# A segment maximum rewritten from chunks and a late gather into a walk over groups and blocks, with 244 steps in an attention walk and another order of two fronts

## The chip, the cores and the metric

The kernel runs on one core of a Trainium2 chip. The metric is device time in microseconds (us), the median of several runs. The engines are TensorE (PE in the rows, PEld its weight loads), VectorE (DVE), ScalarE (ACT), GpSimd (POOL) and SyncE (SP); each works through its own queue of instructions in order, and semaphores join them. Both ScalarE and SyncE also issue DMAs here, and GpSimd issues every indirect DMA (gathers and scatters by a list of row numbers).

## The reference

A graph network of four layers on N = 6250 nodes with D = 128 features and E = 100000 edges. Edges are sorted by `dst`, which is drawn as `floor(6250 * u**2)`, so that low nodes have many edges and high ones few; `src` is random.

```
h = relu(layernorm(x));  x = x + log_softmax(sage(elu(sage(h))))          # two SAGE convolutions, segment means over dst
h = relu(layernorm(x));  x = x + batchnorm(h1 + ffn(h1)),  h1 = batchnorm(h + gat4(h))   # 4 heads, mean over heads
h = relu(layernorm(x));  x = x + prelu(gat2(h))                           # 2 heads of 64
h = relu(layernorm(x));  x = x + relational(h)

def relational(h):                    # the last layer
    msg[e] = h[src[e]] @ W[rel[e]] + b[rel[e]]          # 4 relations
    agg = segment_max(msg, dst);  agg = 0 where a node has no edge
    return h @ W[4] + b[4] + agg
```

An attention layer scores each edge from a term of its source and one of its target, takes a softmax over the edges of each target and sums the weighted sources.

## The kernel before

**Sizes.** P = 128. Nodes are NT = 49 blocks (`tiles`) of 128. The padded edge list has ET = 784 tiles of 128 edges. GT = 7 tiles make a group (GE = 896 edges); there are GN = 112 groups. A *walk* goes through the pairs of group and node block that meet in the sorted list: SN = GN + NT − 1 = 160 steps. Each step has one group of gathered rows and one block of nodes; it moves on either to the next group or to the next block. GpSimd gathers the groups into a ring of RG = 8 groups, and a group's place is freed when its last step has used it.

**The stages.** (1) Two SAGE walks (`walk_pass`, line 899) of 160 steps; GpSimd gathers from `h_tab`, then from `sage_tab` (L919). Per step DVE builds a one-hot of targets (L1056) and PE sums the rows by it, 14 matmuls (L1194). `group_col` and `block_col` hold each step's group and block per partition, for the two table gathers after group LAP = 2, and `retire_walk` the step at which each group's place comes free. (2) A first front (`project`, line 585, with `front` at 1489 and `post` at 1500): in 7 groups of 7 blocks it subtracts the logarithm, takes the layernorm and multiplies by the score weights; `nodeval` receives the products, and GpSimd scatters them, one of 49 scatters per block, into `start1_rows` (L620). (3) The first attention walk (from line 1600) goes by groups of QT = 4 tiles: QN = 196 groups, QN + NT − 1 = 244 pairs, rounded up to QS = 248 steps in QWN = 31 windows of QW = 8. SP stores each finished block to `gat_tab` and `total_tab` (L1646), one store pair for each of the 248 steps. (4) Batchnorm and feed-forward. (5) The second attention's front (`front` at 2400, `post` at 2404), in which ScalarE takes the square root (L830) and the normalised rows and copies the products out; scatters again at L620. (6) The second attention walk. (7) The last front (2853) and products, which write `y_tab`, the rows of all four relations' products for every node. (8) The last pass.

**The order inside `project`.** DVE makes the norms of groups 0 and 1. Then, in each step i, with `starts` given (stages 2 and 5), it waits for product(i), copies it in `post` and then makes norm i + 2; without `starts` (stage 7) norm i + 2 comes first (lines 633 to 638). PE's `turn` of group i + 1 stands before the product of group i (stage 2) or in its middle (stages 5 and 7). In stage 2 the products of seven blocks fill one PSUM area in turn; in stages 5 and 7 four banks take one block's product each (`banks`, line 595).

**The last pass before** (`edge_pass`, line 397, called at 2880). The 784 tiles go in CT = 4 at a time, 196 chunks, in an unrolled loop over NB = 4 buffers. Per chunk, ScalarE copies four columns of `y_idx` to `slot` (L514), which lets GpSimd gather four tiles of `y_tab` (L422); PE transposes them into `pa` (L495); DVE runs a segmented maximum along the edges (L471), where `mask` is a row from `cut_row` that starts each segment anew; PE transposes it back (L505), ScalarE copies it (L525) and issues the write of 512 rows to `scan_rows` (L531). The mask is loaded by SP. Behind the whole loop GpSimd gathers, for each block, the row of every node's last edge from `scan_rows` (`gather_results`, line 549, L557, indices `last_idx`), DVE adds groups of seven blocks to `x` (L2890) and SP stores them (L2899).

The core of it:

```
for t in range(CT):                                    # PE, L495
    ins = nc.tensor.transpose(to, rows(s, t), ident[:, :])
...
v.tensor_tensor_scan(scan_t[:, b, :], mask[:, c, :], pa[:, b * CE:(b + 1) * CE],
                     scan_t[:, 1 - b, CE - 1:CE], op0, op1)          # DVE, L471
```

`last_idx`, the index of each node's last edge, is made between the two SAGE walks in a small block that also makes `start_idx` (from line 1443).

## Time and profile before

| | us |
|---|---|
| median of 3 runs (lowest, highest) | 5873.93 (5870.14, 5876.07) |
| the profiled execution's own time | 5876.16 |
| its span | 5874.4 |
| busy in the span: PE / PEld / DVE / ACT / POOL | 3278.1 / 2756.8 / 2906.4 / 1827.9 / 3903.4 |
| granted TensorE clock, mean over the span | 0.728 |
| first SAGE walk, first gather starts | 58.0 |
| first front, first scatter starts | 2099.3 |
| last pass, first gather of `y_tab` starts | 4816.0 |
| last pass, last gather of `y_tab` starts | 5793.4 |

How to read it: the span is what the profiler recorded of one execution, from its first to its last instruction; the execution's own time holds the 1.8 us around it. Busy times are sums over the whole kernel and mix stages with different limits, so no engine's share says by itself what a stage waits for. The granted clock is a share of 2.4 GHz; 1.0 and 0.5 are TensorE's two levels, and a mean between them is a mixture in time.

### The profile page before, as it was taken

The page shows a single profiled execution, that of the slowest core. Times are in us where ns is not written, and L with a number is a line of the kernel's source. Part 1 is how long each engine was busy: PE and PEld are TensorE (multiplying, and loading weights), DVE is VectorE, ACT ScalarE, POOL GpSimd, SP SyncE. Part 2 cuts the span into 40 slices and gives each one's busy share as a digit, 9 for nine tenths or more (in the row PEclk, how much of TensorE's full clock was granted, in tenths as well). Part 3 has the DMA queues.
Part 4 walks back from the last instruction along what each step waited for, and adds up shares of the span by engine and source line. Part 5 has one row for each costly group of instructions (what it writes and reads, how often), then busy time and mean ns, then how long its engine had stood idle before and what let it go on. Part 6 is the DMA issues. An engine that isn't in the chain of part 4 may idle for free. (4 is left out here: it accounts for less than half of the span.)

```text
span 5874.4 us, 89970 instructions
## 1 busy us (share of the span) xinstructions
PE 3278.1 (56%) x15772; PEld 2756.8 (47%) x15773; DVE 2906.4 (49%) x7625; ACT 1827.9 (31%) x6493; POOL 3903.4 (66%) x4083
## 2 busy tenths in 40 slices
PE   3444555545555525889999894244555563334332
PEld 3444455444555523677777644233445533333331
DVE  4233344434455656788888852344555652222221
ACT  2111111111122213666666653233344441111110
POOL 4777777677777747777776003777777517777776
PEclk9667777766677756999999995566677785555555
DMA  4222222211111112344444211222222134444443
GB/s 122 61 62 63 63 65 66 72 53 52 53 53 52 53 41 78 111 113 117 119 117 113 95 46 31 52 53 54 53 53 52 38 111 130 133 132 130 131 133 107
DMA packets 441899, 474.71 MB, mean 81 GB/s; under 512 B 131954, under 2 KB 337214, under 8 KB 441695
## 3 DMA queue, kind: packets, MB, share of 16 engines
q0 software_dynamic: 130464, 264.37, 17.1%
q1 hardware_dynamic: 184116, 146.31, 8.3%
q10 hardware_dynamic: 127227, 63.09, 3.6%
q14 instruction: 69, 0.57, 0.0%
q8 instruction: 23, 0.38, 0.0%
HBM read 315.46 MB, written 157.97 MB: 81 GB/s over the span
## 5 line engine op out<-in xcount | busy, mean ns | idle before, releaser
L1194 PE MATMUL pa<-arena,weighted 128*128 x4480 | 860.0, 367 | 855.8 <-POOLq L913 511.2
L1194 PEld LDWEIGHTS pa<-arena,weighted 128*128 128x128 f32 x4480 | 795.4, 273 | 909.4 <-issue 909.2
L422 POOL DMA_INDIRECT arena<-y_tab,slot x784 | 739.8, 944 | 398.7 <-issue 209.4
L1607 POOL DMA_INDIRECT arena<-t_tab,src_idx x784 | 777.5, 992 | 265.7 <-issue 216.0
L919 POOL DMA_INDIRECT arena<-h_tab,src_idx x784 | 742.8, 947 | 308.1 <-issue 221.9
L2490 POOL DMA_INDIRECT arena<-t_tab,src_idx x784 | 753.3, 961 | 244.9 <-issue 224.6
L919 POOL DMA_INDIRECT arena<-sage_tab,src_idx x784 | 739.8, 944 | 262.4 <-issue 216.1
L471 DVE TENSOR_TENSOR_SCAN scan_t<-mask,scan_t,pa 128x512 f32<-128x512 bf16 x196 | 250.9, 1280 | 737.1 <-PE pa L495 737.1
L495 PE MATMUL pa<-ident,arena 128*128 128x128 f32 x784 | 218.3, 434 | 603.9 <-DMA arena<-y_tab,slot 603.9
L495 PEld LDWEIGHTS pa<-ident,arena 128*128 128x128 f32 x784 | 140.1, 217 | 681.9 <-DMA arena<-y_tab,slot 430.8
L2731 PE MATMUL pa<-weighted 128*128 128x130 f32 x2240 | 422.6, 364 | 21.0 <-ACT weighted L2809 11.0
L2731 PEld LDWEIGHTS pa<-weighted 128*128 128x128 f32 x2240 | 392.7, 271 | 34.4 <-issue 19.7
L620 POOL DMA_INDIRECT start_rows<-nodeval,start_idx x98 | 98.5, 1005 | 455.1 <-DVE nodeval L2405 372.6
L1056 DVE TENSOR_TENSOR weighted<-pd,rel 128x896 f32<-128x896 f32 x320 | 348.3, 1089 | 51.8 <-issue 47.2
L1064 DVE SCALAR_TENSOR_TENSOR scan_t<-scan_t,alpha,pa 128x130 f32<-128x130 f32 x320 | 110.5, 345 | 503.7 <-PE pb L1201 326.6
L1963 PE MATMUL pa<-weighted 128*128 128x264 f32 x992 | 321.2, 406 | 55.4 <-ACT weighted L2036 35.9
L1239 ACT COPY out_rows<-pb 128x128 f32<-128x128 f32 x320 | 84.6, 264 | 831.5 <-PE pb L1201 700.5
L2036 ACT ACTIVATE weighted<-arena,weighted 128x128 f32 x992 | 322.3, 390 | 62.1 <-POOLq L1598 47.2
L1963 PE MATMUL pa<-arena,weighted 128*128 128x264 f32 x992 | 306.5, 391 | 50.7 <-DVE arena L1769 38.9
L2809 ACT ACTIVATE weighted<-arena,weighted 128x64 f32 x1280 | 323.0, 335 | 19.8 <-ACT weighted L2803 0.2
L525 ACT COPY out_rows<-pb 128x512 f32<-128x512 f32 x196 | 114.7, 585 | 689.4 <-PE pb L505 689.3
L2036 ACT ACTIVATE arena<-arena 128x128 f32 x992 | 312.8, 389 | 14.9
(522 smaller groups left out, 6559.9 us busy)
## 6 DMA issues: line engine op xcount, KB each, us to landing
gat_tab<-out_rows SPq DMA_DIRECT2D x248, 260.0 KB
scan_rows<-out_rows ACTq DMA_DIRECT2D x196, 256.0 KB, 3.7
arena<-t_tab,src_idx POOLq DMA_INDIRECT x1568
mask<-cut_row SPq DMA_DIRECT2D x196, 128.0 KB, 3.1
arena<-h_tab,src_idx POOLq DMA_INDIRECT x784
arena<-sage_tab,src_idx POOLq DMA_INDIRECT x784
y_tab<-arena SPq DMA_DIRECT2D x49, 256.0 KB, 2.3
arena<-y_tab,slot POOLq DMA_INDIRECT x784, 2.8
```

What stands on the lines that cost most here:

```text
L422: nc.gpsimd.indirect_dma_start(out=rows(c, t), out_offset=None, in_=table[:, :], in_offset=bass.IndirectOffsetOnAxis(ap=slot[:, c, t:t + 1 ...
L471: v.tensor_tensor_scan(scan_t[:, b, :], mask[:, c, :], pa[:, b * CE:(b + 1) * CE], scan_t[:, 1 - b, CE - 1:CE], op0, op1).then_inc(chunk_s ...
L495: ins = nc.tensor.transpose(to, rows(s, t), ident[:, :])
L919: nc.gpsimd.indirect_dma_start(out=rows[:, g % RG * GT + t, 0:D], out_offset=None, in_=table[:, :], in_offset=bass.IndirectOffsetOnAxis(ap ...
L1056: v.tensor_tensor(hot[b].rearrange("p (t n) -> p t n", n=P), node_row.unsqueeze(1).broadcast_to([P, GT, P]), at.unsqueeze(2).broadcast_to( ...
L1194: ins = nc.tensor.matmul(pa[:, b * CE:b * CE + RW], hot[b][:, t * P:(t + 1) * P], ring[:, bass.ds(start + t * RW, RW)], start=(t == 0), st ...
L1607: nc.gpsimd.indirect_dma_start(out=rows[:, g % QR * QT + t, :], out_offset=None, in_=t1_tab[:, :], in_offset=bass.IndirectOffsetOnAxis(ap= ...
L1963: nc.tensor.matmul(pa[:, b * CE:b * CE + HALF], one, flow1[b][:, t * YW:t * YW + HALF], start=(t == 0), stop=(t == QT - 1))
L2036: ins = nc.scalar.activation(flow1[b][:, at:at + D], ring1[:, bass.ds(start + t * TW, D)], ACT.Copy, scale=flow1[b][:, t * YW + 2 * D + hd ...
L2490: nc.gpsimd.indirect_dma_start(out=rows[:, g % RB * GT + t, :], out_offset=None, in_=t2_tab[:, :], in_offset=bass.IndirectOffsetOnAxis(ap= ...
L2731: ins = nc.tensor.matmul(pa[:, b * CE:b * CE + BW], hot2[b][:, t * P:(t + 1) * P], flow[b][:, t * BW:(t + 1) * BW], start=(t == 0), stop=( ...
L2809: ins = nc.scalar.activation(flow[b][:, at:at + HD], ring2[:, bass.ds(start + t * BW + hd * HD, HD)], ACT.Copy, scale=flow[b][:, at + HD:a ...
```

## The change

**1. The last pass becomes a walk of 160 steps.** `edge_pass`, `gather_results`, `scan_rows`, `last_idx` and `slot` go. For each pair of group and block, step i:

- GpSimd gathers the 112 groups of seven tiles into the ring of 8, waits for the ring (`group_freed`), and gathers two tables of the nodes' last edges (`last_rows`) behind group 2.
- ScalarE issues the mask's load for step i + 2, copies the back-transposed group out of PSUM (`keep_back`), issues the store of a finished block, and copies step i + 2's group from the ring to a flat buffer (`stage_group`).
- PE transposes group i + 1 (`turn`), multiplies the one-hot of step i − 1 with the kept rows (`select`, f32, into `pd`), and transposes the scanned group back (`back`).
- DVE scans, adds `pd` of step i − 2 to the block's rows in `x`, makes the carry (the last value, kept where the next step goes on with the next group) and builds the one-hot of last edges (`build`).
- SP counts the steps down and frees the ring's places.

New code of PE, ScalarE and DVE (`after(engine, c, n)` waits for the n-th event of c):

```diff
+                def turn(s, b):
+                    after(pe, edge_staged, s + 1)
+                    after(pe, edge_scanned, s - 1)
+                    for t in range(GT):
+                        ins = nc.tensor.transpose(turned_ps[b][:, t * P:(t + 1) * P], staged_t[b][:, t * P:(t + 1) * P], ident[:, :])
+                    ins.then_inc(edge_turned.sem, 1)
+                def back(s, b):
+                    after(pe, edge_scanned, s + 1)
+                    after(pe, edge_kept, s)
+                    for t in range(GT):
+                        ins = nc.tensor.transpose(back_ps[:, t * P:(t + 1) * P], run_t[b][:, t * P:(t + 1) * P], ident[:, :])
+                    ins.then_inc(edge_back.sem, 1)
+                def select(s, b):
+                    after(pe, edge_kept, s + 1)
+                    after(pe, hot_built, s + 1)
+                    after(pe, block_added, s)
+                    for t in range(GT):
+                        ins = nc.tensor.matmul(last_ps, hot[b][:, t * P:(t + 1) * P], kept_t[b][:, t * P:(t + 1) * P],
+                                               start=(t == 0), stop=(t == GT - 1))
+                    ins.then_inc(block_summed.sem, 1)
+                def body(i, b):
+                    if inside(i + 1):
+                        turn(i + 1, 1 - b)
+                    if inside(i - 1):
+                        select(i - 1, 1 - b)
+                    if inside(i):
+                        back(i, b)
...
+                def stage_group(s, b, start, need):
+                    after(act, edge_turned, s - 1)
+                    wait_apart(act, group_landed.sem, group_landed.past(need))
+                    nc.scalar.copy(staged_t[b].rearrange("p (t d) -> p t d", d=D),
+                                   ring[:, bass.ds(start, GT * RW)].rearrange("p (t w) -> p t w", w=RW)[:, :, 0:D]
+                                   ).then_inc(edge_staged.sem, 1)
+                def load_mask(s, b, need):
+                    after(act, edge_scanned, s - 1)
+                    act.dma_start(mask_t[b], cut_row[0:1, bass.ds((need - 1) * GE, GE)].broadcast_to([P, GE])).then_inc(mask_loaded[b].sem, 16)
+                def keep_back(s, b):
+                    after(act, edge_back, s + 1)
+                    after(act, block_summed, s - 1)
+                    nc.scalar.copy(kept_t[b], back_ps).then_inc(edge_kept.sem, 1)
+                def store(s, j):
+                    after(act, block_added, s)
+                    after(act, block_stored, s * 16)
+                    act.dma_start(out[bass.ds(j * P, P), :], x[:, bass.ds(j, 1), :].rearrange("p j d -> p (j d)")
+                                  ).then_inc(block_stored.sem, 16)
+                def body(i, b):
...
+                    if inside(i) and inside(i + 2):
+                        load_mask(i + 2, b, need)
+                    if inside(i):
+                        keep_back(i, b)
+                    if inside(i - 2):
+                        store(i - 2, j)
+                    if inside(i) and inside(i + 2):
+                        stage_group(i + 2, b, start, need)
...
+                def scan(s, b):
+                    after(dve, edge_turned, s + 1)
+                    after(dve, mask_loaded[b], (s - b) * 8 + 16)
+                    after(dve, edge_back, s - 1)
+                    after(dve, carry_ready, s)
+                    v.tensor_tensor_scan(run_t[b], mask_t[b], turned_ps[b], carry_t[b], ALU.add, ALU.max).then_inc(edge_scanned.sem, 1)
+                def carry_on(s, b):
...
+                def build(s, b):
+                    after(dve, block_summed, s - 1)
...
+                def body(i, b):
+                    if inside(i):
+                        scan(i, b)
+                    if inside(i - 2):
+                        add(i - 2, b)
+                    if inside(i):
+                        carry_on(i, b)
+                        build(i, b)
```

On GpSimd and SP:

```diff
+                for g in range(GN):
+                    if g >= RG:
+                        pool.wait_ge(group_freed.sem, group_freed.past(g - RG + 1))
+                    for t in range(GT):
+                        nc.gpsimd.indirect_dma_start(
+                            out=edge_rows[:, g % RG * GT + t, 0:D], out_offset=None, in_=y_tab[:, :],
+                            in_offset=bass.IndirectOffsetOnAxis(ap=y_idx[:, g * GT + t:g * GT + t + 1], axis=0)
+                        ).then_inc(group_gathered[g % RG].sem, 16)
...
+                with sp.Fori(0, GN) as g:
+                    n = sp.value_load(retire_walk[0:1, bass.ds(g, 1)], min_val=1, max_val=SN)
+                    wait_apart(sp, edge_staged.sem, edge_staged.past(n))
+                    sp.sem_inc(group_freed.sem, 1)
```

**2. The first attention walk has 244 steps.** `QL = QN + NT - 1`; the last window has four steps (`fine_steps`), and counts and stores go to QL. Its columns get names of their own (`group_col1`, `block_col1`), so that those of the 160-step walk live on to the last pass.

**3. `project` makes norm i + 2 ahead of the wait for product(i) in all fronts.** The `post` of group i then stands behind three norms instead of two at its start.

```diff
-QS = -(-(QN + NT - 1) // QW) * QW
+QL = QN + NT - 1
+QS = -(-QL // QW) * QW
...
-                with sp.Fori(0, QS // 2) as pair:
+                with sp.Fori(0, QL // 2) as pair:
...
                     def step(i, b, left):
-                        if left > 1 and starts is None:
+                        if left > 1:
                             front(dve, i + 2)
                         dve.wait_ge(group_product.sem, group_product.past(i + 1))
                         post(dve, i, b)
-                        if left > 1 and starts is not None:
-                            front(dve, i + 2)
```

**4. Smaller ones.** The small block between the SAGE walks makes only `start_idx`: four DVE instructions and a transpose fewer. In the setup a few memsets and the load of padding rows into `scan_rows` go.

**How the rows of the queues move.** In the last pass, PE's queue before (the loop over chunks; `pa` takes the chunk that is turned, `pb` the scanned one that is turned back):

```order
L495 MATMUL pa<-ident,arena 128x128 x4
L502 REGISTER_ALU
L503 REGISTER_ALU
L505 MATMUL pb<-ident,scan_t 128x128 x4
L495 MATMUL pa<-ident,arena 128x128 x4
```

And now, inside the loop of the walk (`staged_t` is `arena`, `run_t` and the one-hot are `weighted`, `kept_t` is `arena`; L2839 is `turn`, L2854 `select`, L2846 `back`):

```order
L2839 MATMUL pb<-ident,arena 128x128 x7
L668 REGISTER_ALU x2
L2854 MATMUL pd<-arena,weighted 128x128 x7
L668 REGISTER_ALU
L2846 MATMUL pc<-ident,weighted 128x128 x7
L668 REGISTER_ALU
L2839 MATMUL pa<-ident,arena 128x128 x7
L668 REGISTER_ALU
L2854 MATMUL pd<-arena,weighted 128x128 x7
L2846 MATMUL pc<-ident,weighted 128x128 x7
```

Two kinds of bursts of four became three of seven, in the order turn, select, back; the select stands between the next group's turn and this group's back.

ScalarE's queue in the last pass before (L525 copies the chunk that PE turned back, L514 stages the next indices):

```order
L525 COPY out_rows<-pb 128x512
L531 ISA
L531 DMA scan_rows<-out_rows 128x4x128
L514 ISA
L514 COPY slot<-y_idx 128x4
```

And now, one step of the walk's loop (`alpha` holds the table with each step's block, ring place and group; L2881 is the mask's load, L2886 `keep_back`, L2891 the store, L2875 `stage_group`):

```order
L676 TENSOR_LOAD alpha
L668 REGISTER_ALU
L2881 ISA
L2881 DMA mask<-cut_row 128x896
L668 REGISTER_ALU
L2886 COPY arena<-pc 128x896
L668 ISA
L2891 ISA
L2891 DMA out<-x 128x128
L352 REGISTER_ALU
L2875 ISA
L2875 COPY arena<-arena 128x896
```

The copy into the flat buffer (L2875), for which PE's next turn waits, stands behind the copy out of PSUM (L2886), for which PE's select waits, and behind the store's issue.

DVE's queue at the end of the first front before (the last three groups; L1494 to L825 are one norm, L1501 is `post`):

```order
L1501 COPY nodeval<-pc 128x56
L1494 TENSOR_TENSOR x<-arena,stat 128x896
L810 BN_STATS row_stats<-x 128x6 x7
L813 BN_AGGR moments<-row_stats 128x2 x7
L818 TENSOR_SCALAR ln_stat<-moments 128x7
L819 TENSOR_TENSOR arena<-x,moments 128x896
L821 RECIPROCAL moments<-ln_stat 128x7
L825 SCALAR_TENSOR_TENSOR h<-arena,moments 128x896
L825 SCALAR_TENSOR_TENSOR weighted<-arena,moments 128x896
L1501 COPY nodeval<-pb 128x56
L1501 COPY nodeval<-pc 128x56
```

And now (L1288 to L631 are one norm, L1295 is `post`):

```order
L1288 TENSOR_TENSOR x<-arena,stat 128x896
L616 BN_STATS row_stats<-x 128x6 x7
L619 BN_AGGR moments<-row_stats 128x2 x7
L624 TENSOR_SCALAR ln_stat<-moments 128x7
L625 TENSOR_TENSOR arena<-x,moments 128x896
L627 RECIPROCAL moments<-ln_stat 128x7
L631 SCALAR_TENSOR_TENSOR h<-arena,moments 128x896
L631 SCALAR_TENSOR_TENSOR weighted<-arena,moments 128x896
L1295 COPY nodeval<-pc 128x56
L1295 COPY nodeval<-pb 128x56
L1295 COPY nodeval<-pc 128x56
```

One `post` went from ahead of the last norm to behind it.

## Rows read from the trace of the kernel before

**Rows 1.** The page's first line.

```profile
span 5874.4 us, 89970 instructions
```

**Rows 2.** Instructions by line: ns min/median/max, starts of the first and last, count.

```profile
L422 POOL DMA_INDIRECT arena<-y_tab,slot x784: 940/944/962, 4816.0 to 5793.4; - x196
L919 POOL DMA_INDIRECT arena<-h_tab,src_idx x784: 940/944/1769, 58.0 to 1055.3; - x196
```

**Rows 3.** Timeline, last pass, one chunk: start us, us, instruction [idle before <-releaser].

```profile
5308.27 1.11 PE L495 MATMUL pa<-ident,arena 128*128 128x128 f32 x4 [4.70 <-DMA arena<-y_tab,slot]
...
5309.58 1.28 DVE L471 TENSOR_TENSOR_SCAN scan_t<-mask,scan_t,pa 128x512 f32<-128x512 bf16 x1 [5.27 <-PE pa L495]
...
5310.37 0.58 ACT L525 COPY out_rows<-pb 128x512 f32<-128x512 f32 x1 [5.27 <-PE pb L505]
...
5311.64 0.19 ACT L514 COPY slot<-y_idx 128x4 int32 x1 [0.69 <-ACT out_rows L525]
```

**Rows 4.** End of the kernel: late gathers by line, and the last store (timeline).

```profile
L557 POOL DMA_INDIRECT arena<-scan_rows,last_idx x49: 940/944/947, 5806.1 to 5866.0; - x49
...
5870.19 0.44 SPq L2899 DMA_DIRECT2D out<-x  x1
```

**Rows 5.** Stretches: length, busy PE (x), PEld, DVE, ACT, POOL, clock, DMA share, GB/s.

```profile
600.00:1000.00 400.00, 218.63 (x1272) 201.05 (x1273) 169.21 (x521) 63.90 (x224) 302.48 (x321) 0.79 0.23 65
1600.00:1950.00 350.00, 200.12 (x1096) 189.79 (x1094) 193.55 (x513) 76.88 (x322) 264.46 (x281) 0.75 0.18 53
2400.00:3100.00 700.00, 634.13 (x2835) 514.16 (x2834) 596.22 (x1551) 468.22 (x1716) 529.79 (x539) 0.99 0.41 116
4816.00:5794.00 978.00, 382.77 (x1556) 304.98 (x1556) 249.57 (x195) 150.99 (x388) 739.38 (x784) 0.50 0.47 130
```

**Rows 6.** Timeline of SP's queue, end of the first attention walk.

```profile
3320.42 0.34 SPq L1646 DMA_DIRECT2D gat_tab<-out_rows  x1
...
3334.45 0.34 SPq L1646 DMA_DIRECT2D gat_tab<-out_rows  x1
```

**Rows 7.** Timeline of DVE and POOL in the first front.

```profile
2092.28 1.08 DVE L825 SCALAR_TENSOR_TENSOR weighted<-arena,moments 128x896 f32<-128x896 f32 x1
...
2098.22 0.22 DVE L1501 COPY nodeval<-pc 128x56 f32 x1 [4.85 <-PE pc L672]
...
2104.88 1.08 DVE L825 SCALAR_TENSOR_TENSOR weighted<-arena,moments 128x896 f32<-128x896 f32 x1
...
2099.27 1.24 POOL L620 DMA_INDIRECT start_rows<-nodeval,start_idx  x1 [40.89 <-DVE nodeval L1501]
...
2160.40 0.98 POOL L620 DMA_INDIRECT start_rows<-nodeval,start_idx  x1 [2.19 <-DVE nodeval L1501]
...
2177.13 0.98 POOL L620 DMA_INDIRECT start_rows<-nodeval,start_idx  x1 [0.30 <-issue]
```

**Rows 8.** Timeline of ScalarE, front of the second attention, two groups.

```profile
3585.87 0.21 ACT L830 ACTIVATE ln_stat<-ln_stat 128x7 f32<-128x7 f32 x1 [4.02 <-DVE ln_stat L787]
...
3600.07 0.21 ACT L830 ACTIVATE ln_stat<-ln_stat 128x7 f32<-128x7 f32 x1 [4.02 <-DVE ln_stat L787]
```

**Rows 9.** Groups of instructions: count | busy us, mean ns | idle before; the second by line.

```profile
L1194 PE MATMUL pa<-arena,weighted 128*128 x4480 | 860.0, 367 | 855.8 <-POOLq L913 511.2
...
L1056 DVE TENSOR_TENSOR weighted<-pd,rel x320: 1072/1092/1093, 113.0 to 2059.6; 128x896 f32<-128x896 f32 x160
...
L691 ACT COPY weighted<-pa 128x896 f32<-128x896 f32 x21 | 19.0, 905 | 50.8 <-PE pa L650 50.8
...
L1740 DVE TENSOR_TENSOR_SCAN arena<-keep,carry,weighted 112x896 f32<-112x896 f32 x4 | 8.2, 2064 | 0.0
```

**Rows 10.** Timeline of PE: end of the second SAGE walk, and first front.

```profile
2052.20 1.83 PE L1194 MATMUL pa<-arena,weighted 128*128 x14 [0.72 <-DVE weighted L1056]
...
2057.11 2.80 PE L1194 MATMUL pa<-arena,weighted 128*128 x14 [2.75 <-DVE scan_t L1064]
...
2086.54 1.76 PE L650 MATMUL pa<-ident,weighted 128*128 128x128 f32 x7 [16.96 <-DVE weighted L825]
```

More of the change, by code:

```diff
@@ L564, in results_gathered @@
-        def results_gathered():
-            for b in range(2):
-                group_rows[b].base += 16 * NG * ((groups + 1 - b) // 2)
-            group_here.base += groups
         def stage(s):
@@ L583, in group_steps, with project @@
                 step(i, i % 2, min(groups - 1 - i, 2))
-        def project(ns, front, by_tile, by_group, post, begin=None, scalar_front=None, scalar_post=None, gathers=None, store=None,
+        def project(ns, front, by_tile, by_group, post, begin=None, scalar_front=None, scalar_post=None, store=None,
                     buffers=None, starts=None):
@@ L608, in project @@
             with nc.Block() as block:
-                if gathers is not None:
-                    @block.gpsimd
-                    def _(pool):
-                        gathers(pool)
                 if starts is not None:
@@ L1431, in build @@
         cleared.base += 3
-        idx_staged.base += 1
+        iota_made.base += 1
         turned.base += 1
@@ L2886, in _ @@
             @block.vector
             def _(dve):
-                with dve.Fori(0, groups) as i:
-                    dve.wait_ge(group_here.sem, group_here.past(i + 1))
-                    nc.vector.tensor_tensor(middle(x, i), middle(x, i), middle(g, i), ALU.add).then_inc(group_kept.sem, 1)
-            @block.sync
-            def _(sp):
-                for i in range(groups):
-                    sp.wait_ge(group_kept.sem, group_kept.past(i + 1))
-                    j, full = i * NG, NG if i < groups - 1 else NG - 1
-                    sp.dma_start(out[j * P:(j + full) * P, :].rearrange("(j p) d -> p j d", p=P), x[:, j:j + full, :]
-                                 ).then_inc(stored.sem, 16)
-                sp.dma_start(out[(NT - 1) * P:N, :], x[0:NL, NT - 1, :]).then_inc(stored.sem, 16)
-                sp.wait_ge(stored.sem, stored.past(16 * (groups + 1)))
+                v = nc.vector
```

368 lines of the change are left out of this document (162 added, 206 removed).

## The prediction

> **What bounds the kernel now.** I read the page first, then the chain that ended last (which here says only that GpSimd's gathers end it), then each stage's start and end from the gathers' own rows, and last the timeline of one step per stage, to see which wait ends last there. The page's span [rows 1] is one profiled execution whose own time was 5876.16 us; the median of the three runs, 5873.93 us, is 2.2 us below it. Time is summed against 5876.2 and 2.2 us are taken off at the end.
>
> *The last pass.* The 784 gathers of `y_tab` start from 4816.0 to 5793.4, one per 1.25 us [rows 2]: 0.94 us of work and 0.30 us of issue. What follows them is light: a chunk's four transposes take 1.11 us, its scan 1.28 us, its copy 0.58 us, and PE then stands 4.70 us for the next gather [rows 3]. So this pass is bound by GpSimd. Behind it come 49 more gathers, from 5806.1 to 5866.0, the last add and the last store [rows 4]. From the first gather to the end of the span it is 5874.4 − 4816.0 = 1058.4 us, of which 80 lie behind the last `y_tab` gather.
>
> *TensorE's clock.* In the two SAGE walks PE is busy 55% and 57% of the time and is granted 0.79 and 0.75 of 2.4 GHz; in the attention walk it is busy 91% and has 0.99; in the last pass 39% and 0.50, which is 1.2 GHz throughout [rows 5].
>
> *The other places.* The first attention walk ends with five stores from 3320.42 to 3334.45, 3.51 us apart [rows 6]. In the first front DVE holds GpSimd's scatters back: `nodeval` waits 4.85 us for PE, and only then does the next norm begin [rows 7]. In the front of the second attention ScalarE waits 4.02 us in each group of 14.2 us for statistics that DVE takes only behind `post` [rows 8].
>
> **The change, part by part.**
>
> *1. The tail goes.* The 49 gathers, their adds and the 196 writes of `scan_rows` go; the new pass stores each block as it is done. If the 112 groups of seven gathers were still the bound, the pass would be like the first SAGE walk, whose 784 gathers with the same two table gathers run from 58.0 to 1055.3, 997.3 us [rows 2], plus about 18 us for the last step and the store: 1015 us, 43 less than now. That is the hope of the change; next is what stands against it.
>
> *2. A step is a closed circle.* The walk has 112 + 49 − 1 = 160 steps, one for each pair of group and block. The order of PE's queue is turn(i+1), select(i−1), back(i), and ScalarE's is keep(i), store(i−2), stage(i+2). So back(i) releases keep(i), behind it on ScalarE comes stage(i+2), that releases turn(i+2), and behind it on PE stand select(i) and back(i+1), in this order. Nothing in it can run ahead: one step costs at least one lap. The lap, from rows: keep, a PSUM copy of 128x896, 0.905 us [rows 9]; from its end to the next copy with a DMA issue between, 0.69 us [rows 3]; stage, a copy of the same size, taken as 0.91; 28 PE instructions (7 transposes, 7 transposes, 7 f32 matmuls of two instructions each: the SAGE walk's 4480 are 14 in each of 320 steps [rows 9]); and four handovers, by my estimate 0.3 in all. At the low level four transposes take 1.11 us [rows 3] and seven 1.76 [rows 10], so an instruction is (1.76 − 1.11)/3 = 0.217 us and a burst's start 0.24. At the high level fourteen take 1.83 us [rows 10], between 0.114 without the start and 0.131 with it; I take 0.118, since bursts follow each other here. The lap is then 2.8 + 28 × 0.118 = 6.1 us with the clock always high, and 2.8 + 28 × 0.217 = 8.9 us with it always low.
>
> DVE is beside this circle: a scan of 896 columns is 2.06 us from SBUF [rows 9] or 1.28 × 896/512 = 2.24 from PSUM's row, the one-hot 1.09 [rows 9], three small ones about 1 us: 4.4 us of a lap. The register load for `block_walk` hides under the scan. The mask is issued two steps ahead. These cost nothing as long as the lap is over 4.4 us.
>
> *3. Which clock.* With a lap of about 7 us PE is busy 60%, just over the SAGE walks' 55 to 57%, so I take their clock, 0.78: high for a share h with 0.5 + 0.5h = 0.78, h = 0.56. An instruction then takes 1/(0.56/0.118 + 0.44/0.217) = 0.148 us, and the lap is 2.8 + 28 × 0.148 = 6.95 us. Rows speak against a clock that stays high in such a walk: a burst of 14 took 1.83 us, PE stood for 2.75 us soon after it, and the next 14 took 2.80 us, most of them at the low level [rows 10]; a lap here has the same gap of 2.8 us.
>
> *4. The pass.* A group arrives every 7 × 1.25 = 8.74 us. `dst` is 6250 u², so at share f of the edge list a group crosses 49 × 2f/112 = 0.875f block borders and takes 1 + 0.875f steps. Below f = (8.74/6.95 − 1)/0.875 = 0.29 gathers bound the walk, above it the lap does: 0.29 × 112 × 8.74 = 288 us, then 112 × 0.71 + 49 × (1 − 0.29²) = 124 steps × 6.95 = 861 us, and 16 us for last step, store and end: 1165 us. The tables delay the first step (in the first SAGE walk 55 us from the first gather to the first one-hot [rows 2, 9]; here about 45, without the own terms); the ring of eight groups covers it and the first groups, one step each, win it back. Against 1058.4 that is **+107 us**. POOL will then wait for the ring.
>
> *5. Attention walk of 244 steps.* Four padding steps at the end go: 4 × 3.51 = **−14.0 us** [rows 6]. No cover is lost: the next block waits for the last store in either case.
>
> *6. Fronts.* With norm(i+2) ahead of the wait for product(i), the third norm begins at 2093.4, where the second ends, and not at 2098.4; it takes 7.5 us, so `nodeval` of group 0 comes at 2101.1 instead of 2098.4 and the first scatter at 2102.0 [rows 7]. From there groups follow DVE's 7.7 us, less than GpSimd's 7 × 1.287 = 9.0 (the last 14 scatters start from 2160.40 to 2177.13), so the 49 scatters run through: 2102.0 + 48 × 1.287 + 0.6 for slower first ones = 2164.4 for the last start instead of 2177.1: **−13 us**. Late next is the scatter itself. In the other front five of seven norms lose their wait of 4.02 us; ScalarE still gives 0.25 to the handover: 5 × 3.75 = **−18.7 us**, and its period, 14.2 − 3.75 = 10.4, stays above the scatter's 9.0 [rows 8]. Bounds: from 0, if ScalarE's copies or a DMA take the wait's place, to 25. The last projection starts no scatters and had this order before. The small index table loses a transpose and four DVE instructions: 0 to −1 us, taken as 0.
>
> Sum: 5876.2 + 107 − 14.0 − 13 − 18.7 = 5937.5; less 2.2: **5935 us**.
>
> **The rivals.**
>
> *A. The clock stays high in the last pass.* The lap is 6.1 us and gathers bound it up to f = 0.49: 0.49 × 112 × 8.74 = 480, then 94 steps × 6.1 = 574, and 16: 1070 us, and 5876.2 + 12 − 45.7 − 2.2 = **5840 us**, faster. The point from which it decides is a lap of 6.4 us (1103 us of pass, the 45.7 us of the other parts used up). For it: the walk's bursts are longer than SAGE's. Against it: the pair of bursts in [rows 10], and that no walk with gaps had more than 0.79 [rows 5]. The Trainium skill (TensorE: Matmul & The Clock Gate, section "HAM oscillation — how this bites in real kernels") puts the loss of the high level down to idle gaps beyond a certain length, so that bursts with short gaps stay warm; by that rule, applied to this lap, the result would be this rival's. The trace disagrees at a gap of 2.75 us.
>
> *B. The clock sinks further, or handovers are longer.* With a lap of 7.5 us: bound from f = 0.19: 185 + 138 × 7.5 + 16 = 1236, so +178: **6006 us**; with 8.0 us it is 6080, and with the low clock throughout 160 × 8.9 + 61 = 1485 gives 6255. For it: 1.2 GHz in this place before [rows 5]. Against: that was 39% busy.
>
> *C. The circle is broken somewhere that I don't see and GpSimd bounds the pass:* 1015 us, 5876.2 − 43 − 45.7 − 2.2 = **5785 us**.
>
> *D. The fronts give nothing* because something else was late: 5935 + 32 = 5967, inside the range.
>
> **How the numbers follow.** Forecast (lap 6.5 to 7.2, 5880 to 5970): 0.55. A (lap under 6.5): 0.15. B: 0.20. C: 0.05. D: 0.05. A change below 0.2%, 12 us, can't be told from none in this kernel. Faster by more than that is C and most of A: 0.18; within it 0.05; slower the rest: 0.77. The range goes from A's time, 5840, to a lap of 7.7 us, 6040; C and the far part of B, together some 0.15, are left out.
>
> **What would show it.** Right: GpSimd's `y_tab` gathers spread over some 1080 us with idle time released by SP's `group_freed`; keep, stage, turn, select and back follow each other without a pause on PE and ScalarE from about a third of the pass on; a lap of 6.5 to 7.2 us; a clock of 0.75 to 0.85; fewer than 20 us behind the last gather's own step. The attention walk shows 244 stores. In the first front scatters follow each other without a gap; in the second ScalarE's idle time before the square root is gone. Wrong: gathers that still start every 1.25 us to the end (then C), a clock over 0.95 (A), or a DVE that is busy over 90% in the pass, which would mean that the scan and not the circle sets the step.

## The result, and the profile after

The changed kernel takes 5928.53 us (median of 4 runs, 5924.81 to 5931.29), the kernel before beside it 5872.03 us (5870.0 to 5876.07). The ratio is 1.0095 with a 95% interval of 1.0077 to 1.0112: slower by about 56 us. The forecast was 5935.

Source view of the changed kernel, gathers, scatters and stores: ns min/median/max, starts of the first and last.

```profile
L725 POOL DMA_INDIRECT arena<-h_tab,src_idx x784: 940/944/1764, 56.9 to 1054.2; - x196
L725 POOL DMA_INDIRECT arena<-sage_tab,src_idx x784: 940/944/1094, 1078.4 to 2056.1; - x196
L430 POOL DMA_INDIRECT start_rows<-nodeval,start_idx x98: 980/982/1860, 2100.4 to 3613.2; - x98
L1405 POOL DMA_INDIRECT arena<-t_tab,src_idx x784: 939/944/2392, 2174.2 to 3214.7; - x196
L1444 SPq DMA_DIRECT2D gat_tab<-out_rows x244: 332/336/393, 2278.8 to 3312.2; - x122
L2288 POOL DMA_INDIRECT arena<-t_tab,src_idx x784: 940/944/2573, 3620.5 to 4611.0; - x196
L2709 POOL DMA_INDIRECT arena<-y_tab,y_idx x784: 938/944/1810, 4770.4 to 5825.7; - x196
```

The kernel before has at these places, by the same view:

```profile
L1607 POOL DMA_INDIRECT arena<-t_tab,src_idx x784: 938/944/2406, 2184.4 to 3222.9; - x196
L1646 SPq DMA_DIRECT2D gat_tab<-out_rows x248: 337/339/394, 2289.5 to 3334.4; - x124
L2490 POOL DMA_INDIRECT arena<-t_tab,src_idx x784: 940/944/2569, 3664.0 to 4654.7; - x196
```

With [rows 2] these give the difference stage by stage:

| from ... to | before | after | difference | forecast |
|---|---|---|---|---|
| start to the attention walk's first gather (first front) | 2184.4 | 2174.2 | −10.2 | −13 |
| that gather to the walk's last store (244 steps) | 1150.0 | 1138.0 | −12.0 | −14.0 |
| that store to the second attention walk's first gather (second front) | 329.6 | 308.3 | −21.3 | −18.7 |
| that gather to the first of `y_tab` | 1152.0 | 1149.9 | −2.1 | 0 |
| first gather of `y_tab` to the end of the span | 1058.4 | 1157.1 | +98.7 | +107 |
| sum of the spans | 5874.4 | 5927.5 | +53.1 | +61.3 |

**The last pass.** Timeline of the changed kernel, one step, from one `keep` to the next (start us, us, instruction, idle before it and who ended that):

```profile
5405.92 0.91 ACT L2886 COPY arena<-pc 128x896 f32<-128x896 f32 x1 [5.12 <-PE pc L2846]
...
5406.83 0.94 ACT L2875 COPY arena<-arena 128x896 f32 x1
...
5407.82 1.04 PE L2839 MATMUL pb<-ident,arena 128*128 128x128 f32 x7 [2.02 <-ACT arena L2875]
...
5408.65 3.20 PE L2854 MATMUL pd<-arena,weighted 128*128 128x128 f32 x14
...
5408.90 2.08 DVE L2782 TENSOR_TENSOR_SCAN weighted<-mask,alpha,pb 128x896 f32<-128x896 bf16 x1 [2.01 <-PE pb L2839]
...
5411.65 1.12 PE L2846 MATMUL pc<-ident,weighted 128*128 128x128 f32 x7
...
5412.88 0.91 ACT L2886 COPY arena<-pc 128x896 f32<-128x896 f32 x1 [5.12 <-PE pc L2846]
```

These are the five members of the circle in the forecast's order, with no pause between them. From the start of keep it is 0.91 us to the start of stage, 0.99 more to turn, 0.83 to select, 3.00 to back, 1.12 to back's end and 0.11 to the next keep; 6.96 in all. The work of GpSimd and DVE and the pauses of ScalarE (5.12 us) and PE (2.02 us) lie inside that time. Over the pass the median of the 159 intervals between two starts of `keep` is 6.98 us. GpSimd meets a full ring in the second half only: behind the table gathers its starts are 1.25 us apart up to 5541.9, where the first gap for a full ring comes.

Groups of the changed kernel (busy us, mean ns | idle before, and who ended it):

```profile
L2886 ACT COPY arena<-pc 128x896 f32<-128x896 f32 x160 | 145.0, 906 | 813.3 <-PE pc L2846 797.8 <-DVE weighted L2782 10.4 <-PE pd L2854 5.1
...
L2875 ACT COPY arena<-arena 128x896 f32 x160 | 150.0, 937 | 47.5 <-POOLq L2703 39.5 <-DMA out<-x 2.5
...
L2839 PE MATMUL pb<-ident,arena 128*128 128x128 f32 x560 | 95.9, 321 | 168.4 <-ACT arena L2875 168.4
```

ScalarE waits 797.8 us for PE's back and PE waits for ScalarE's stage; for a gathered group (the POOLq part) stage waits 39.5 us in the whole pass. In the chunk shown of the kernel before, PE's wait was for a gather [rows 3]. The windows (columns as in [rows 5]) show what clock goes with it:

```profile
4830.00:5000.00 170.00, 108.82 (x641) 103.23 (x640) 84.83 (x115) 42.28 (x46) 128.35 (x137) 0.79 0.33 92
5400.00:5600.00 200.00, 139.68 (x821) 132.57 (x822) 107.99 (x146) 54.26 (x59) 140.46 (x150) 0.78 0.34 92
```

The same view for the parts of the lap above (keep and stage, turn, select, back) shows where in it the clock was low:

```profile
5405.92:5407.82 1.90, 0.00 (x0) 0.00 (x1) 0.96 (x1) 1.84 (x2) 1.59 (x2) 1.00 0.35 104
5407.82:5408.65 0.83, 0.83 (x7) 0.83 (x8) 0.00 (x0) 0.00 (x0) 0.53 (x2) 0.98 0.01 0
5408.65:5411.65 3.00, 3.00 (x17) 3.00 (x16) 2.08 (x1) 0.00 (x0) 2.39 (x3) 0.50 0.48 142
5411.65:5412.80 1.15, 1.11 (x8) 0.88 (x7) 0.54 (x3) 0.00 (x0) 0.85 (x2) 0.84 0.19 57
```

### The profile page after: what moved, and what is told of

It reads as the page before. It is cut to its first block and busy times, and to the rows that moved or that the text cites. A ratio compares the mean times of both kernels' runs of the same rounds, so it can differ in the third digit from the quotient of the medians.

```text
span 5927.5 us, 98732 instructions
## 1 busy us (share of the span) xinstructions
PE 3654.2 (62%) x18635; PEld 3174.2 (54%) x18636; DVE 3238.8 (55%) x8215; ACT 1958.6 (33%) x6380; POOL 3864.0 (65%) x4036
## 5 line engine op out<-in xcount | busy, mean ns | idle before, releaser
L2709 POOL DMA_INDIRECT arena<-y_tab,y_idx x784 | 741.1, 945 | 471.1 <-issue 223.4
L2854 PE MATMUL pd<-arena,weighted 128*128 128x128 f32 x2240 | 445.5, 381 | 2.0 <-ACT arena L2886 2.0
L2854 PEld LDWEIGHTS pd<-arena,weighted 128*128 128x128 f32 x2240 | 432.1, 295 | 2.5 <-ACT arena L2886 2.5
L2886 ACT COPY arena<-pc 128x896 f32<-128x896 f32 x160 | 145.0, 906 | 813.3 <-PE pc L2846 797.8
L1763 PE MATMUL pc<-weighted 128*128 128x256 f32 x976 | 297.1, 387 | 0.0
```

The costliest lines, as they stand in the source:

```text
L1763: ins = nc.tensor.matmul(pc[:, b * CE:b * CE + 2 * D], one, flow1[b][:, t * YW + HALF:(t + 1) * YW], start=(t == 0), stop=(t == QT - 1))
L2709: nc.gpsimd.indirect_dma_start(out=edge_rows[:, g % RG * GT + t, 0:D], out_offset=None, in_=y_tab[:, :], in_offset=bass.IndirectOffsetOnAx ...
L2854: ins = nc.tensor.matmul(last_ps, hot[b][:, t * P:(t + 1) * P], kept_t[b][:, t * P:(t + 1) * P], start=(t == 0), stop=(t == GT - 1))
```

## The experiments

All experiments but e5, which starts from the kernel before, start from the changed kernel. All of them, e5 too, also check the bounds of the loaded group numbers that their waits use, one register instruction more behind each such load, so the first run is that alone: the control.

**Control (e1).**

```diff
-            return [nc.s_assert_within(value, low, high, skip_runtime_bounds_check_because=why)
+            return [nc.s_assert_within(value, low, high) if low > 0 else
+                    nc.s_assert_within(value, low, high, skip_runtime_bounds_check_because=why)
                     for value, (low, high) in zip(values, bounds)]
```

> The changed kernel, with one more register instruction behind each loaded group number that a wait uses (a check of its bounds); every other experiment has it too, so this run is what they are compared with. Theory (the circle back, keep, stage, turn, select sets the step, 6.93 us in the changed kernel's profile): the check lies on ScalarE ahead of the mask's load, in its idle time of 5.1 us, and costs nothing: 5925 to 5935 us. Rival (ScalarE's queue has no slack): 160 steps by 0.05 to 0.1 us, 8 to 16 us more, 5937 to 5945.

Measured: 5935.69 us (5933.05 to 5937.55). Its pass is 5935.8 − 4778.4 = 1157.4 us, as without the check, so the idle time in the pass hides it, as the theory has it. But the kernel is 7 us slower, between the theory's range and the rival's: its `y_tab` gathers start 8.0 us later. The last gather of the first attention walk is 5.9 us later already (3220.6 against 3214.7). Which engine the check holds up there isn't settled.

**Stage ahead of keep (e2).**

```diff
                     if inside(i) and inside(i + 2):
                         load_mask(i + 2, b, need)
+                        stage_group(i + 2, b, start, need)
                     if inside(i):
                         keep_back(i, b)
                     if inside(i - 2):
                         store(i - 2, j)
-                    if inside(i) and inside(i + 2):
-                        stage_group(i + 2, b, start, need)
```

> ScalarE's order becomes mask(i+2), stage(i+2), keep(i), store(i-2); nothing else moves. Theory of the circle: stage and turn leave it, what is left is back 7 instructions, keep 0.91 us, select 14 instructions, with handovers of about 0.5 in all: 21 x 0.148 + 0.91 + 0.5 = 4.5 us a lap, DVE's 4.3 and PE's 28 x 0.148 = 4.1 near it; a lap of 4.5 to 5.3 us. A group arrives every 8.74 us and meets at most 1.9 steps, so GpSimd bounds nearly all of the pass: 1015 to 1050 us instead of 1157, and the kernel 5785 to 5825 us. Rival 1 (PE's own work at a low clock sets the step, not the order): the pass stays within 20 us, 5910 to 5935. Rival 2 (the wait for a group's landing now holds keep(i) back, so that everything queues behind the gathers): a pass of 1100 or more, over 5870.

Measured: 5781.67 us (5776.69 to 5787.46), 154 us less than the control, ratio to the kernel before 0.9844 (0.9828 to 0.9861). The pass is 1004.4 us. Both rivals fall; the time and the pass lie a little below the theory's ranges (5785 to 5825, 1015 to 1050).

**Select behind back (e3).**

```diff
                     if inside(i + 1):
                         turn(i + 1, 1 - b)
-                    if inside(i - 1):
-                        select(i - 1, 1 - b)
                     if inside(i):
                         back(i, b)
+                    if inside(i - 1):
+                        select(i - 1, 1 - b)
```

> PE's order becomes turn(i+1), back(i), select(i-1); ScalarE's stays. Theory of the circle: select leaves it and lies beside keep and stage: 14 instructions x 0.148 + 0.91 + 0.94 + 0.95 for issue and handovers = 4.9 us a lap, if select's 2.1 to 3.1 us fit beside the 2.8 of ScalarE: a lap of 4.9 to 5.5 us, the pass mostly bound by GpSimd, 1015 to 1055 us, the kernel 5785 to 5830 us. Rival 1 (PE's work sets the step): 5910 to 5935. Rival 3 (the wait is DVE's: select(i-1) later makes add and the next one-hot late): a lap over 6 us, over 5870.

Measured: 5779.12 us (5774.54 to 5783.1), ratio 0.9837 (0.9821 to 0.9853). Source view of its gathers:

```profile
L2710 POOL DMA_INDIRECT arena<-y_tab,y_idx x784: 940/945/994, 4774.7 to 5755.2; - x196
```

980.5 us from the first to the last, 783 intervals of 1.252 us: GpSimd runs at its own pace to the end, and 20.5 us follow. The pass is 5775.7 − 4774.7 = 1001.0 us. Timeline of a stretch in which two steps of one group follow each other:

```profile
5455.62 0.91 ACT L2887 COPY arena<-pc 128x896 f32<-128x896 f32 x1 [1.92 <-issue]
...
5456.53 0.94 ACT L2876 COPY arena<-arena 128x896 f32 x1
...
5457.52 0.98 PE L2840 MATMUL pb<-ident,arena 128*128 128x128 f32 x7 [0.46 <-ACT arena L2876]
...
5458.34 0.93 PE L2847 MATMUL pc<-ident,weighted 128*128 128x128 f32 x7
...
5459.11 1.73 PE L2855 MATMUL pd<-arena,weighted 128*128 128x128 f32 x14
...
5459.39 0.91 ACT L2887 COPY arena<-pc 128x896 f32<-128x896 f32 x1 [1.92 <-PE pc L2847]
```

Select now runs beside ScalarE's copies, and this lap is 3.77 us, so the theory's 4.9 to 5.5 was too long: here the 28 PE instructions ran at the high level (turn 0.98, back 0.93, select 1.73 us). The kernel's time is again somewhat below the range.

**Both orders (e4).** The two diffs together.

> Both orders at once. Theory: no circle through both queues is left, a lap is the largest of DVE's 4.3 us, PE's 28 x 0.148 = 4.1 and back, keep and their handovers; GpSimd bounds the whole pass: 1010 to 1030 us, the kernel 5780 to 5805 us, at most 20 us below the better of the two single orders. Rival: they share one hidden bound (the scan's chain of carry on DVE), and both together give what one gives alone, at a pass over 1050.

Measured: 5780.73 us (5779.44 to 5785.32), ratio 0.9841 (0.9825 to 0.9858). Its gathers take 4776.6 to 5757.5, again 980.9 us. The three orders can't be told apart, and the reason is the theory's, not the rival's: either one breaks the circle, and GpSimd bounds the pass then. Over the last 53 of the 159 laps, where most groups are used in two steps, the medians between two keeps are 3.87, 4.10 and 4.05 us (e2, e3, e4) against 6.98.

**Fronts alone (e5).** The kernel before with the order of `project.step` changed.

```diff
-                        if left > 1 and starts is None:
+                        if left > 1:
                             front(dve, i + 2)
                         dve.wait_ge(group_product.sem, group_product.past(i + 1))
                         post(dve, i, b)
-                        if left > 1 and starts is not None:
-                            front(dve, i + 2)
```

> The kernel before with nothing but the order in project.step: norm(i+2) ahead of the wait for product(i) in all fronts. By the changed kernel's trace the first front gave 8.9 us and the second 20.3 us between first and last scatter, and 1.0 ahead of the first. Theory (the three parts of the change add up, each at its own place): 30 us less than before, and up to 8 us more for the bounds checks that the control showed, so 5840 to 5855 us. Rival (part of the gain in the fronts came from other parts, such as the smaller index table or the 244 steps): less than 15 us of gain, over 5860.

Measured: 7405.41 us against 7396.11 for the kernel before on the same chip, ratio 1.0014 (0.9997 to 1.0031). e5 to e8 came to a chip, and e9 and e10 to another, on which the kernel before itself takes 7396 and 7405 us, with pauses of some 8 us scattered over the stages; I call both the slower chips. Their absolute times say nothing about the chips of e1 to e4. By this measure the sum is a miss: no gain is seen there, and why is open. What its trace does show is the first front by itself: 66.62 us from its first to its last scatter, as in the changed kernel (66.51) and not as before (77.86, 11.35 more; the 8.9 of the expectation was wrong). So that part comes from the order alone. The second front took 80.08 us there, between the two (86.66 and 66.29) and with the chip's pauses in it, so nothing follows for that one.

**A second copy on ScalarE (e6).**

```diff
+                    nc.scalar.copy(h[:, b * GT:(b + 1) * GT, :],
+                                   ring[:, bass.ds(start, GT * RW)].rearrange("p (t w) -> p t w", w=RW)[:, :, 0:D])
                     nc.scalar.copy(staged_t[b].rearrange("p (t d) -> p t d", d=D),
```

> The control with one more copy of the group (0.94 us, into a buffer that nobody reads) ahead of stage_group's own on ScalarE. Theory of the circle: every step is longer by the whole copy, 159 x 0.94 = 150 us, and up to 20 more if TensorE's granted clock sinks with the longer pauses: 6080 to 6110 us. Rival (ScalarE has slack, its share in the pass is only 25%): under 5950.

**A second one-hot on DVE (e7, e10).**

```diff
+                    v.tensor_tensor(h[:, b * GT:(b + 1) * GT, :],
+                                    node_row.unsqueeze(1).broadcast_to([P, GT, P]),
+                                    at.unsqueeze(2).broadcast_to([P, GT, P]), ALU.is_equal)
```

> The control with a second one-hot of 1.09 us in every step on DVE (into a buffer that nobody reads) ahead of the true one. Theory of the circle: DVE is beside it; in the changed kernel's profile the one-hot ends 1.77 us before select begins and the next scan waits 2.0 us for PE, so 1.09 us more is hidden: 5925 to 5945 us, as the control. Rival (DVE's chain of scan, add, carry and one-hot sets the step): 160 x 1.09 = 174 us more, 6100.

> The same kernel as in the run of the second one-hot, on another chip (there the median interval between two keeps was 7.04 us against 6.98 in the control). Theory (DVE is beside the circle with 1.8 us to spare before select): 5930 to 5945 us, as the control's 5936. Rival (DVE sets the step): 6100.

Measured, all on the slower chips: the copy 7779.29 us (7771.11 to 7783.71), the one-hot 7686.84 (7676.95 to 7700.31) and 7693.43 (7676.68 to 7706.48). On the same chip 0.94 us more on ScalarE costs 92 us more (e6 against e7) than 1.09 us more on DVE. The control hasn't run on those chips, so the ranges of the three expectations can't be tested on the kernels' times; the steps can be set against it, between the pauses. Timeline of e6, from one keep to the next:

```profile
7560.09 0.91 ACT L2889 COPY arena<-pc 128x896 f32<-128x896 f32 x1 [6.37 <-PE pc L2847]
...
7561.00 0.94 ACT L2876 COPY h<-arena 128x896 f32 x1
...
7561.85 0.93 ACT L2878 COPY arena<-arena 128x896 f32 x1
...
7567.90 0.91 ACT L2889 COPY arena<-pc 128x896 f32<-128x896 f32 x1 [5.12 <-PE pc L2847]
```

And of e7, from one keep to the next:

```profile
7567.79 0.91 ACT L2890 COPY arena<-pc 128x896 f32<-128x896 f32 x1 [5.11 <-PE pc L2850]
...
7568.32 1.09 DVE L2795 TENSOR_TENSOR h<-pd,rel 128x896 f32<-128x896 f32 x1
...
7569.32 1.08 DVE L2798 TENSOR_TENSOR weighted<-pd,rel 128x896 f32<-128x896 f32 x1
...
7574.76 0.91 ACT L2890 COPY arena<-pc 128x896 f32<-128x896 f32 x1 [5.11 <-PE pc L2850]
```

7.81 us with the second copy, 6.97 with the second one-hot. The medians of all laps under 9 us, which leaves the pauses out, are 7.81 and 7.03 us, against 6.98 in the control of e1. The second copy takes 0.85 us on ScalarE, from its start to the next copy's, and the lap is 0.84 longer: stage is in the circle with its full length; the one-hot is beside it.

**PE kept busy (e8, e9, e12).**

```diff
                     ins.then_inc(edge_back.sem, 1)
+                    for t in range(8):
+                        nc.tensor.transpose(turned_ps[b][:, 0:P], ident[:, :], ident[:, :])
```

> The control with eight transposes of the identity behind each back on PE, into the PSUM buffer that the next turn overwrites; PE stands 2.0 us there, and eight cost 0.94 us at the high level and 1.74 us at the low one, so they delay nothing by themselves. Theory (28 instructions of the circle cost 0.148 us each because TensorE is granted 0.77 of its clock in a walk with pauses, and a busier PE is granted more): a granted clock of 0.9 or more in the pass, a lap of 6.1 to 6.5 us, a pass of 1060 to 1095, the kernel 5835 to 5875 us. Rival (the 2.80 us bursts have another cause, or eight transposes do not move the clock): a clock below 0.82 and 5925 to 5950 us.

> The same kernel as in the run of eight transposes behind each back, on another chip: where that ran, the kernel before itself took 7396 us and all stages stood for DMAs, so the lap could only be read there between the pauses (control 6.98 us; a last third at 6.6). Theory (the clock follows how busy PE is, and the 28 instructions of the circle follow the clock): a clock of 0.9 or more in the pass, a lap of 6.1 to 6.5, the kernel 50 to 100 us below the control's 5936. Rival (eight transposes do not move the clock enough, and stand in the way of the next turn where they run at the low level): a clock below 0.82, within 15 us of the control or slower.

Measured on the slower chips: 7678.55 (7671.33 to 7707.22) and 7677.22 us (7670.64 to 7681.39), 8 us below e7 and 16 below e10: as whole kernels inconclusive. The granted clock from 7000 to 7200 us was 0.77 in e8 and 0.70 in e7, so neither expectation of 0.9 or more is met. Behind the last gather, though, the pauses end, and there the transposes do what the theory says: the last 12 laps before the final two take 5.36 us on average at a granted clock of 1.00 in e8 and e9, and 6.86 us at 0.77 in e7 and e10.

> The control once more, beside the next run. If it lands on the chip on which the kernel before took 7396 to 7405 us: the base for what ran there. Theory of the circle: the second one-hot (7687 and 7693 us there) was hidden, so the control is within 25 us of that, 7665 to 7700, and the second copy (7779 us) costs 80 to 115 us more than the control, less than its 150 since pauses for DMAs cover part of it. Rival (the one-hot was not hidden): a control at or below 7610 us. If it lands on the first chip: 5930 to 5940 us.

> Eight transposes behind each back, on the same chip as the control beside it. The two runs so far (7679 and 7677 us, select's 14 instructions in 1.73 us in a quarter of the steps and over 3.0 in another, a clock of 0.77 against 0.70 with the second one-hot) say that eight are too few to hold the high level. On the slower chip: within 20 us of the control. On the first chip: theory 5835 to 5900, rival 5925 to 5950; by those runs between both, 5880 to 5930.

Measured, on a third chip, where the kernel before takes 5873.45 us: the control 5933.28 us (5931.1 to 5935.9), as expected, and with eight transposes more in each step 5802.30 (5801.55 to 5805.42), ratio to before 0.9881 (0.9865 to 0.9898). 160 × 8 transposes that compute nothing save 131 us. The middle value I gave from the slower chips' runs, 5880 to 5930, is a miss; the theory's ranges, 5835 to 5875 and later to 5900, were too high as well. Windows of e12 (columns as in [rows 5]):

```profile
5000.00:5200.00 200.00, 136.67 (x1018) 130.02 (x1019) 103.53 (x141) 52.56 (x57) 151.24 (x161) 0.89 0.36 94
5400.00:5600.00 200.00, 153.34 (x1321) 144.54 (x1320) 134.23 (x185) 68.22 (x74) 150.99 (x160) 1.00 0.40 107
```

And of the control beside it (e11):

```profile
5000.00:5200.00 200.00, 137.26 (x802) 130.31 (x801) 106.94 (x145) 53.43 (x58) 150.96 (x161) 0.77 0.36 95
5400.00:5600.00 200.00, 140.47 (x825) 133.35 (x824) 109.45 (x146) 53.43 (x58) 141.34 (x150) 0.77 0.36 93
```

Timeline of e12, one lap:

```profile
5505.61 0.91 ACT L2889 COPY arena<-pc 128x896 f32<-128x896 f32 x1 [3.48 <-DVE weighted L2783]
...
5506.52 0.94 ACT L2878 COPY arena<-arena 128x896 f32 x1
...
5507.52 0.98 PE L2840 MATMUL pb<-ident,arena 128*128 128x128 f32 x7 [1.15 <-ACT arena L2878]
...
5508.34 1.73 PE L2857 MATMUL pd<-arena,weighted 128*128 128x128 f32 x14
...
5509.90 0.93 PE L2847 MATMUL pc<-ident,weighted 128*128 128x128 f32 x7
...
5510.94 0.91 ACT L2889 COPY arena<-pc 128x896 f32<-128x896 f32 x1 [3.48 <-PE pc L2847]
```

The same circle in 5.33 us instead of 6.96: ScalarE's part is the same, PE's went from 4.95 to 3.31 us.

## Why the prediction was right, step by step

**The circle: right, and shown.** The step that carried the forecast, a closed lap back, keep, stage, turn, select, stands in the timeline. Two different cuts through it (e2, e3) each give 154 to 157 us, both together give no more, and one copy more in it shows in full while one one-hot more beside it doesn't. Of the signs named, DVE's share (52% of the pass), the clock, the lap and the gathers' wait for the ring came as said; the `y_tab` gathers spread over 1055.3 us where about 1080 was said.

**The lap: 6.95 forecast, 6.98 measured, but by two errors that cancel.**

| term | forecast | measured |
|---|---|---|
| keep, gap, stage, handovers | 0.91 + 0.69 + 0.91 + 0.3 = 2.8 | 0.91 + 0 + 0.94 + 0.16 = 2.01 |
| 28 PE instructions | 28 × 0.148 = 4.15 | 0.83 + 3.00 + 1.12 = 4.95, 0.177 each |

The 0.69 us of [rows 3] lay between two copies with a store's issue between that waited for the first; here the store on ScalarE's queue starts in the middle of `keep` (at 5406.19 in the lap above) and hides. And the step from the granted clock to a price per instruction failed: from the clock of a stretch, 0.78, I took 0.56 as the share of PE's *busy* time at the high level. It is the share of *all* time, PE's pauses among it. In the lap above, the pause while ScalarE copies and turn had the high level (clock 1.00 and 0.98; 0.83 us for turn's 7), select the low (0.50; 3.00 us for 14, 0.214 each), back a mixture (0.84; 1.12 us for 7). Which burst the low level hits differs from lap to lap: over the pass turn takes 0.98 to 1.76 us in most laps, select 1.73 to 3.20, back 0.93 to 1.76. But it hardly ever falls into a pause. By the trace's clock records from 5200 to 5900 us, 317 of the 700 us are at the low level, and PE is busy in 314 of these; it is busy for 489 us in all, so 64% of its busy time is low, where the forecast had 44%. PE's share of the time, forecast at 60%, was 70% for the same reason. The forecast's own prices were right at both ends: 0.118 at the high level is 3.31/28 in e12, and 0.217 at the low is select's 0.214.

**The pass: 1165 forecast, 1157.1 measured, again by errors that cancel.** The first keep starts at 4819.85, 49.5 us behind the first gather, and the last at 5921.23, 159 steps of 6.93 us on average. Of the forecast's three terms, the first, 36 steps bound by the gathers, was 288 us; the 37th keep starts 312.0 us behind the first gather. The tables keep the first turn back until 44 us behind the first gather, when GpSimd has started four and a half groups, so the first steps run off that lead. Then, from the 11th to the 30th stage, ten stages wait for a group, 16.5 us in all, and no later one does. So the delay of the tables was won back in part only. The second term, 124 laps of 6.95 = 861 us, was too long: the 123 laps behind the 37th keep take 838.8 us, 6.82 each, since some laps take 5.33 (see below). The third, 16 us for the end, is 6.3 from the last keep. (The cuts aren't quite at the same places, as stage runs two steps ahead of keep.)

**The 244 steps: −14.0 forecast, −12.0 measured.** Between the first and the last store the four steps took 11.5 us off, not 14. Where 2.5 us of the walk went isn't settled, and no run has this part alone.

**First front: −13 forecast, −10.2 measured.** The third norm ahead of `post` and the gapless scatters came as forecast. The term that failed is the scatter's 1.287 us: the 49 took 66.51 us from first to last start, not 62.4, since six lasted over 1.2 us (see below). The forecast had taken its 1.287 from the last 14 scatters and 0.6 us for slower first ones. 1.1 of the 10.2 us was there before the first SAGE walk had begun.

**Second front: −18.7 forecast, −21.3 measured.** From first to last scatter it is 66.29 us instead of 86.66, 20.4 less, so the waits of [rows 8] went: of the six before the square root, five (19.4 us together) are gone, and ScalarE's period is 9.6 to 10.1 us where 10.4 was forecast. Beyond that, 2.1 us between the first gather of the second attention walk and the first of `y_tab` were not forecast and have no known cause. e5 confirms the first front's share by itself, the second front's not: that one rests on the trace of the changed kernel.

**The rivals.** C, the circle broken, was priced 5785 us; e2 to e4 are 5779 to 5782. A, the high clock, was priced 5840 with a lap of 6.1; made true by e12, it gives 5802 with a lap of 5.33, since the fixed part had been taken too long. B, a clock that sinks further or a lap of 7.5 us, fell with 6.98, and D with the fronts' rows of the table. That the clock was low in this pass depends on how PE's work lies in the lap: e12 has a gap of 1.15 us and a clock of 1.00, the control beside it a gap of 2.02 us and 0.77. e12 both shortens the gap and adds work, so these runs don't tell which of the two decides. The Trainium skill (TensorE: Matmul & The Clock Gate, section "HAM oscillation — how this bites in real kernels") explains the loss of the high level by idle gaps between bursts. e12 agrees with it; in the control the clock falls at a gap shorter than those by which that section explains its loss, and there the measurement decides.

## What to carry to other kernels

When an engine does three things per step for different steps of a software pipeline, write down for each what releases it and what stands ahead of it in its queue, and look for a lap that leads through two queues back to itself: its length bounds the step however idle the engines are (here ScalarE 27% and PE 70% busy), and swapping two independent pieces in one queue may remove it, at no cost. Then check which engine's own pace remains. And read a mean granted clock as a share of all time, pauses included, and not of the time in which PE works: here nearly all of the low level fell on PE's work. In such a step work that computes nothing can pay (131 us here), but the swap that opens the circle paid more (154 to 157 us).

## What was not expected of the hardware

**A dense PE pays for useless work.** 1280 transposes made the kernel 131 us faster (e12), since the clock from 5400 to 5600 us rose from 0.77 to 1.00 and PE's part of the lap fell from 4.95 to 3.31 us. The gap before turn fell to 1.15 us with it.

**The clock moves in step with the lap.** In the changed kernel 129 of the 159 laps take 6.9 to 7.1 us, and in the second half of the pass each ninth or tenth takes 5.33 to 5.39 us, the value that most laps of e12 have. In such a lap all of PE's bursts have the high level (around 5450 us: turn 0.98, select 1.73, back 0.93 us). Between two of them the low level moves through the lap: from 5415 to 5443 us the turns take 1.23, 1.37, 1.55, 1.69 and 1.76 us.

**Scatters stand behind DVE.** Timeline of the changed kernel's first front:

```profile
2103.03 1.08 DVE L625 TENSOR_TENSOR arena<-x,moments 128x896 f32<-128x896 f32 x1
2103.11 1.86 POOL L430 DMA_INDIRECT start_rows<-nodeval,start_idx  x1 [0.30 <-issue]
...
2106.78 1.08 DVE L1288 TENSOR_TENSOR x<-arena,stat  x1
...
2106.90 1.82 POOL L430 DMA_INDIRECT start_rows<-nodeval,start_idx  x1 [0.31 <-issue]
```

A scatter that starts 0.08 to 0.17 us behind the start of a DVE instruction with two SBUF inputs takes 1.77 to 1.86 us instead of 0.98 (five of the 49), and these two end 0.86 us after it. One that starts 0.63 us behind takes 1.32 and ends 0.85 after; three that start at the same time or 0.01 us behind take 0.98 as ever. The Trainium skill (SBUF — State Buffer, section "🔬 SBUF: two separate sides") describes a port that such an instruction and a GpSimd instruction that reads SBUF share, and that one of them holds at a time; these rows agree. In this front it cost 4.7 us (49 scatters sum to 52.87 us of work where 49 × 0.982 = 48.1). Before, the 49 sum to 50.29 us, so about half of that is new; that it came because DVE no longer pauses while the scatters run is my reading, and no run tests it.
